# Layer-0 attention: turned keys and P.V sums copied by ScalarE instead of VectorE

## The chip, the core and the metric

One core of a Trainium2 chip runs the whole program. The metric is the device time in microseconds of one execution. Engine names in rows: PE is TensorE (PEld its weight loads), DVE is VectorE, ACT is ScalarE, POOL is GpSimd.

## What is computed

The reference is two transformer-like layers over x of shape (2, 1024, 128). Each layer adds the sum of an attention-like block and a feed-forward block, both fed with the layer-normed x. In layer 0 the two blocks are:

```python
# attention-like block: a small MLP is trained on keys and values, step by step
params, _ = jax.lax.scan(step, (W1, b1, W2, b2), (k, v))   # 1024 gradient steps
q = x @ W_Q
return _mlp(params, q)

# feed-forward block: causal attention with 16 heads of 8, then 4 gated experts
q = _rms(heads(wq), qn_w); k = _rms(heads(wk), kn_w); v = heads(wv)
scores = jnp.einsum('bhqd,bhkd->bhqk', q, k) * HD ** (-0.5)
attn = jax.nn.softmax(jnp.where(causal[None, None], scores, -jnp.inf), axis=-1)
ao = jnp.einsum('bhqk,bhkd->bhqd', attn, v)...
```

Layer 1 has a causal attention with 16 heads of 64 and 8 gated experts. The change concerns the causal attention of layer 0 only, which is the softmax attention over 2 batches, 16 heads, 1024 tokens.

## The kernel before

The program runs in stages: norm and projections (to about 68 us), layer-0 attention together with the training of the small MLP (to about 627 us), the rest of layer 0 (to about 780 us), layer-1 attention and experts (to the end).

The stage of the change works in trips. One trip is one batch and one group of four heads (`HG`), so there are `TRIPS` = 8. A trip has two passes:

- The first pass, `FIRST0`, finds the row maxima. It turns the keys with TensorE transposes (`("tk", half)`, two halves of 512 tokens), turns the queries (`("tq", half)`), multiplies them (`("a", p)`, 48 products), and VectorE takes the maximum of each product (`("mx", p)`, lines 1340 and 1343). The maxima are put beside the queries (`("cb", h)`, line 1346), and the queries are turned again with them (`("tq2", half)`).
- The second pass, `SECOND0`, makes the probabilities: scores again (`("st", n, h)`, 12 blocks of keys by 4 heads, line 1861), an exponential on ScalarE (`("ex", n, h)`, line 964), and the products with the values (`("pv", n)`, line 1878), summed in PSUM bank 6. After blocks 3 and 11 (`LAST`) the sums are complete; they are copied to the tile `ots` (`("oc", half)`, line 1350), turned (`("to", half)`), and VectorE divides them by the sum of the exponentials (`rc` and `zt`, lines 1355 and 1358).

All turns (`tk`, `tq`, `tq2`, `to`, line 1826) write one PSUM bank, `TURN_BANK` = 7, so each waits until the one before has been copied out. The turned keys go to `kta` (`("ka", half)`, line 1327), the turned queries to `qta` and `qtb` by four ScalarE copies of 32 rows each (line 955), each copy from and to the rows 32h to 32h+31 of head h.

In the same queues runs the training of the MLP, one pair of 64-token chunks to a trip: a serial chain of small products (line 1656), a tanh (line 949), and VectorE steps (`sl` line 1242, `grc` line 1251, the differences and their maxima in lines 1295 and 1301 in the first sweep of a chunk, the updates of the state in line 1290).

The order of all this is one written string, `SLOT`, in which every letter takes the next step of the training (`t`), of the first pass of trip s (`f`) or of the second pass of trip s-1 (`s`). Every engine walks the same list and takes what is its own, in that order. Seven full slots run (the first starts near 118 us, the last ends near 587 us); `SLOT_HEAD` before them has no second pass, `SLOT_TAIL` behind them no first pass. The list of one slot begins and ends so:

```python
st.0.0  t.1.base  st.0.1  tk.0  t.1.zc.0  st.0.2  st.0.3  tq.0  copy.tq.0.0  st.1.0  t.1.y.0 ...
... pv.0  tk.1  a.0  a.1  st.2.0  t.1.y.1  a.2  a.3  st.2.1  tq.1 ...
... t.1.zc.4  t.1.kvn  pv.3  a.16  st.5.0  t.1.y.4  st.5.1 ...
... pv.10  tq2.1  copy.tq2.1.0  t.0.dc.4  copy.tq2.1.1  pv.11  copy.tq2.1.2  t.0.up  to.1  copy.tq2.1.3
```

On VectorE a copy stands at `tk` and at `pv.3` and `pv.11`. Who waits for these copies on TensorE (`turn_bank_freed` and `slot`): `tq.0` and `tq.1` wait for `ka` 0 and 1, as the bank has to be free; the products `a` and `st` for the keys; `to.0` and `to.1` for `oc` 0 and 1, and also for the bank; `pv.4` and the next slot's `pv.0` for bank 6.

Of the kernel before, what the change touches and what calls it, by code (L numbers as in the profile page):

```python
# [77 lines left out]
def program(nc, x_in, w0_in, w1_in, out):  # L78
    with ExitStack() as ctx:
# [214 lines left out]
        TURN_BANK = 7  # L294
# [52 lines left out]
        def vector_steps(items):  # L347
            vec = []
            for r in items:
                if r[0] == "tk":  # L350
                    vec.append(("ka", r[1]))
                elif r[0] == "a":
                    vec.append(("mx", r[1]))
                    c, h, i, k = PIECES0[r[1]]
                    if (c, i, k) == (1, TB - 1, 1):
                        vec.append(("cb", h))
                elif r[0] == "pv" and r[1] in LAST:
                    vec.append(("oc", LAST.index(r[1])))
                elif r[0] == "to":
                    vec += [("rc", r[1]), ("zt", r[1])]  # L360
            return vec

        f0_pe = Steps(sem("f0_products"), [r for r in FIRST0 if r[0] != "copy"])
        s0_pe = Steps(sem("s0_products"), SECOND0)
        f0_act = Steps(sem("f0_scalar"), [("qa" if r[1] == "tq" else "qb",) + r[2:] for r in FIRST0 if r[0] == "copy"])
        s0_act = Steps(sem("s0_scalar"), [("ex",) + r[1:] for r in SECOND0 if r[0] == "st"])
        f0_dve = Steps(sem("f0_vector"), vector_steps(FIRST0))
# [521 lines left out]
        def _(act):  # L889
# [47 lines left out]

            def slot(order, s, before):
                for r in order:
# [5 lines left out]
                    elif r[0] == "t" and r[2] == "zc":  # L945
                        _, q, _, k = r
                        src = zh if k else zb
                        wait(act, t_dve, (q, "z", k) if k else (q, "zb"), before if q else s)
                        act.activation(th[:, :, :], src[:, :, :], ACT.Tanh).then_inc(t_act.sem, 1)
                    elif r[0] == "copy":  # L950
                        _, kind, half, h = r
# [14 lines left out]

            slot(SLOT_HEAD, 0, None)
            for i in range(TRIPS // 2 - 1):
                slot(SLOT, i * 2 + 1, i * 2)
                slot(SLOT, i * 2 + 2, i * 2 + 1)  # L970
            slot(SLOT, TRIPS - 1, TRIPS - 2)
            slot(SLOT_TAIL, TRIPS, TRIPS - 1)

# [102 lines left out]
        def _(dve):  # L1076
# [241 lines left out]
            def slot(order, s, before, b, g):  # L1318


                kta_, tmq = kta[:, b, :], tmqs[:, b, :, :]
                for r in order:
                    if r[0] == "t":
                        train_step(before if r[1] else s, *r[1:])
                    elif r[0] == "tk":
                        wait(dve, f0_pe, r, s)
                        dve.tensor_copy(kta_[:, 512 * r[1]:512 * (r[1] + 1)], PS[:, TURN_BANK, :])\
                            .then_inc(f0_dve.sem, 1)
                    elif r[0] == "a":
# [14 lines left out]
                        if (c, i, k) == (1, TB - 1, 1):  # L1344
                            wait(dve, f0_dve, ("mx", r[1]), s)
                            dve.tensor_tensor(tmq[:, 4:8, col], NMH0[:, h, :, 0], NMH0[:, h, :, 1], ALU.min)\
                                .then_inc(f0_dve.sem, 1)
                    elif r[0] == "pv" and r[1] in LAST:
                        wait(dve, s0_pe, r, before)
                        dve.tensor_copy(ots[:, LAST.index(r[1]), :], PS[:, 6, :]).then_inc(s0_dve.sem, 1)  # L1350
                    elif r[0] == "to":
# [278 lines left out]
        def _(pe):  # L1630
# [159 lines left out]
            def turn_bank_freed(order, r, s, before):  # L1790

                turns = [t for t in order if is_turn(t)]
                k = turns.index(r)
                if k == 0:
                    wait(pe, f0_act, ("qb", 1, HG - 1), s, 1)
                    if before is not None:
                        wait(pe, s0_dve, ("zt", 1), before, 1)
                    return
                kind, half = turns[k - 1]
                if kind == "tk":  # L1800
                    wait(pe, f0_dve, ("ka", half), s)
                elif kind == "to":
                    wait(pe, s0_dve, ("zt", half), before)
                else:
                    wait(pe, f0_act, ("qa" if kind == "tq" else "qb", half, HG - 1), s)

            def slot(order, s, before, b):
                for r in order:
                    if r[0] == "t":
                        train_step(before if r[1] else s, *r[1:])  # L1810
                    elif is_turn(r):
# [6 lines left out]
                        elif kind == "tq2":  # L1818

                            wait(pe, f0_dve, ("cb", HG - 1) if half else ("mx", P0_HALF - 1), s)  # L1820
                        elif kind == "to":
                            wait(pe, s0_dve, ("oc", half), before)
                        tm = {"tk": tmk, "to": None}.get(kind, tmqs[:, b, :, :])
# [4 lines left out]
                    elif r[0] == "a":  # L1828
# [5 lines left out]
                        if (i, k) == (4 * c, 0):  # L1834
                            wait(pe, f0_act, ("qa", c, h), s)
                            wait(pe, f0_dve, ("ka", c), s)
                        if p >= 2:
# [6 lines left out]
                    elif r[0] == "st":  # L1844
# [14 lines left out]
                        if n == 0:  # L1859
                            wait(pe, f0_dve, ("ka", 1), before)  # L1860
                        ins = pe.matmul(PS[:, 4 + h % 2, 0:w], kta[:, 1 - b, j * P:(j + 1) * P], qtb[:, h, q0:q0 + w],  # L1861
                                        start=True, stop=True)
                        ins.then_inc(s0_pe.sem, 1)
                    elif r[0] == "pv":
# [4 lines left out]
                        if n == 0:  # L1869
                            pe.wait_ge(s0_values, before + 1)  # L1870
                            wait(pe, s0_dve, ("oc", 1), before, 1)
                        elif j == 0:
                            wait(pe, s0_dve, ("oc", 0), before)
                        if n in DIAG0:
# [284 lines left out]
```

## Time and profile before

| what | us |
|---|---|
| runs | 1507.38, 1503.93, 1507.27; median 1507.27 |
| the profiled execution | 1505.46 |
| its span, first to last instruction | 1503.7 |
| PE busy | 1383.7 (92%) |
| DVE busy | 1103.2 (73%) |
| ACT busy | 784.8 (52%) |

The page gives the busy time of each engine over the span. The views named below read the trace of the same execution: stretches of time with the busy time of each engine, waits by pair of lines, groups of instructions by line and form, and the timeline of one engine, in which a row has its start, its duration, and in brackets the idle time before it with what ended it. A row with "x4" merges four instructions in a row; its duration is that of all four.

### The profile page before, as it was taken

What the parts mean: (1) busy time and instruction counts of PE and PEld (TensorE: products, weight loads), DVE (VectorE), ACT (ScalarE), POOL (GpSimd) and SP (SyncE); (2) the same over time, 40 slices, a digit from 0 to 9 for tenths busy, and PEclk for the clock granted to TensorE, in tenths of its full rate; (3) what the DMA queues carried; (4) which work ended last, traced back from release to release, by engine and by line L of the source; (5) the groups of instructions that cost most, each with busy time, mean ns of one, the idle gap of its engine ahead of it and who ended that gap; (6) DMA issues with size and microseconds to landing.
All of it is one profiled execution on the core that took longest, in us unless ns stands there. A gap on an engine that the chain in (4) does not pass through costs nothing.

```text
span 1503.7 us, 27515 instructions
## 1 busy us (share of the span) xinstructions
PE 1383.7 (92%) x9204; PEld 1055.9 (70%) x9204; DVE 1103.2 (73%) x3389; ACT 784.8 (52%) x1701; POOL 280.3 (19%) x413
## 2 busy tenths in 40 slices
PE   4189999999999999889949999999999999989998
PEld 2167677777767776656627777788787777768887
DVE  3788888989888887452247778887878877855555
ACT  3315464555546555443327666666667666633322
POOL 4001011111101101000043323322222333400000
PEclk9589999999999999989979999999999999989999
DMA  2000000000000000300000000000000000000000
GB/s 96 0 2 1 1 1 1 2 1 1 1 1 2 1 2 1 137 5 0 0 14 1 1 2 1 1 2 1 1 1 2 1 2 1 1 1 1 0 0 28
DMA packets 5612, 12.02 MB, mean 8 GB/s; under 512 B 112, under 2 KB 5232, under 8 KB 5232
## 3 DMA queue, kind: packets, MB, share of 16 engines
q1 hardware_dynamic: 5488, 10.44, 1.9%
q8 instruction: 69, 1.13, 0.3%
q14 instruction: 55, 0.45, 0.1%
HBM read 9.39 MB, written 1.05 MB: 7 GB/s over the span
## 4 chain that ended last, share of the span: by engine, by line
PE 56%; DVE 4%; POOL 1%; ACT 1%; issue 1%; DVEq 0%; ACTq 0%; POOLq 0%
PE PS L2019 9%; PE PS L2033 8%; PE PS L2087 6%; PE PS L2012 5%; PE PS L2011 5%; PE PS L1960 5%; PE PS L2100 4%; PE PS L2046 4%; PE PS L2053 4%; PE PS L1980 2%; PE PS L2061 2%; PE PS L1656 2%; PE PS L1861 1%; PE PS L1878 1%; PE PS L1935 1%
## 5 line engine op out<-in xcount | busy, mean ns | idle before, releaser
L964 ACT ACTIVATE pe_<-PS 128x512 f32<-128x512 f32 (+3 forms) x384 | 176.0, 488 | 152.7 <-PE PS L1861 151.3
L1031 ACT ACTIVATE PN<-PS,NM 128x128 f32<-128x128 f32 (+7 forms) x256 | 189.7, 742 | 106.5 <-DVE NM L1529 52.3
L1529 DVE CUSTOM_DVE_ANT_0 PS<-PS,mask_row 128x128 f32<-128x128 f32 (+7 forms) x256 | 192.6, 773 | 41.9 <-PE PS L2012 38.2
L2011 PE MATMUL PS<-KA,QA 128*128 128x512 f32 (+3 forms) x384 | 161.5, 420 | 15.2 <-DVE KA L1568 14.4
L2019 PE MATMUL PS<-ident,PN 128*128 128x128 f32 x1152 | 170.8, 276 | 1.6 <-ACT PN L1031 1.5
L1841 PE MATMUL PS<-kta,qta 128*128 128x512 f32 (+3 forms) x384 | 146.0, 411 | 7.3 <-DVE tmqs L1340 2.4
L2019 PEld LDWEIGHTS PS<-ident,PN 128*128 128x128 f32 x1152 | 131.8, 141 | 27.7 <-issue 17.4
L1861 PE MATMUL PS<-qtb,kta 128*128 128x512 f32 (+3 forms) x384 | 136.3, 385 | 1.0 <-ACT pe_ L964 0.9
L2012 PE MATMUL PS<-KB,QA 128*128 128x512 f32 (+3 forms) x384 | 129.1, 348 | 0.0
L1340 DVE CUSTOM_DVE_ANT_0 PS<-PS,W 128x128 f32<-128x128 f32 (+3 forms) x256 | 124.7, 496 | 3.6 <-PE PS L1841 2.3
L786 POOL TENSOR_SCALAR_AFFINE_SELECT pe_<-pe_ 128x512 f32<-128x512 f32 x64 | 40.8, 637 | 407.2 <-ACT pe_ L964 407.2
L2011 PEld LDWEIGHTS PS<-KA,QA 128*128 128x128 f32 x384 | 73.6, 192 | 33.4 <-DVE QA L1565 14.5
L1841 PEld LDWEIGHTS PS<-kta,qta 128*128 128x128 f32 x384 | 70.8, 193 | 33.3 <-issue 9.9
L1861 PEld LDWEIGHTS PS<-qtb,kta 128*128 128x128 f32 x384 | 68.6, 190 | 34.3 <-ACT pe_ L964 24.8
L850 POOL CAST KA<-RAW 64x512 fp32r<-64x512 f32 x64 | 46.3, 723 | 243.9 <-ACT RAW L1053 241.5
L1343 DVE TENSOR_REDUCE NMH<-PS 128x1 f32<-128x512 f32 x128 | 87.9, 687 | 4.1 <-PE PS L1841 4.1
L2087 PE MATMUL PS<-QA,w_s 128*128 128x512 f32 x256 | 83.6, 408 | 5.4 <-DVE w_s L1594 5.2
L856 POOL TENSOR_TENSOR KB<-RAW,KA 64x512 fp32r<-64x512 f32 x64 | 87.2, 1363 | 4.4
L1070 ACT ACTIVATE pe_<-PS 128x512 f32<-128x512 f32 x64 | 38.0, 598 | 86.3 <-PE PS L2087 45.7
L2012 PEld LDWEIGHTS PS<-KB,QA 128*128 128x128 f32 x384 | 74.1, 193 | 12.6 <-issue 7.1
L1878 PE MATMUL PS<-pe_,arena 128*32 128x512 f32 (+3 forms) x768 | 81.8, 498 | 0.0
L1039 ACT ACTIVATE PTB<-PS 128x512 f32<-128x512 f32 (+2 forms) x144 | 64.7, 483 | 30.2 <-PE PS L2019 29.2
(253 smaller groups left out, 3103.7 us busy)
## 6 DMA issues: line engine op xcount, KB each, us to landing
W<-w SPq DMA_DIRECT2D x1, 5124.0 KB, 15.8
W<-w SPq DMA_DIRECT2D x1, 2508.0 KB, 10.8
X<-x SPq DMA_DIRECT2D x2, 512.0 KB, 4.8
out<-X SPq DMA_DIRECT2D x1, 1024.0 KB, 5.1
WOZ<-w SPq DMA_DIRECT2D x2, 256.0 KB, 4.2
```

Source lines behind the costliest of these rows:

```text
L964: act.activation(pe_[:, h, n % 2, 0:w], PS[:, 4 + h % 2, 0:w], ACT.Exp, scale=HD0 ** -0.5)\
L1031: act.activation(prob_rows(u, r), scores_of(u), ACT.Exp, bias=NM[:, u:u + 1], scale=-1.0, accum_out=SM[:, r % 2, u:u + 1]).then_inc(score_ ...
L1340: dve.tensor_tensor_reduce(piece, piece, mask_row0[:, 512 - w:512], -1.0, -MASKED, ALU.add, ALU.min, dst).then_inc(f0_dve.sem, 1)
L1529: dve.tensor_tensor_reduce(scores_of(u), scores_of(u), mask_row[:, S - w:S], -HD1 ** -0.5, -MASKED, ALU.add, ALU.min, NM[:, u:u + 1]).then ...
L1841: ins = pe.matmul(PS[:, bank, 0:w], qta[:, h, i * P:(i + 1) * P], kta[:, b, 512 * k:512 * k + w], start=True, stop=True)
L1861: ins = pe.matmul(PS[:, 4 + h % 2, 0:w], kta[:, 1 - b, j * P:(j + 1) * P], qtb[:, h, q0:q0 + w], start=True, stop=True)
L1878: ins = pe.matmul(PS[32 * h:32 * h + 32, 6, q0 - 512 * c:512], tmv[:, j, 32 * h:32 * h + 32], pe_[:, h, n % 2, 0:512 * (c + 1) - q0], star ...
L2011: pe.matmul(piece, query, KA[:, b, h, lo:lo + n], start=True, stop=False)
L2012: ins = pe.matmul(piece, query, KB[:, b, h, lo:lo + n], start=False, stop=True)
L2019: ins = pe.transpose(PS[:, ring_bank[item, r], (j - 4 * k) * P:(j - 4 * k + 1) * P], prob_rows(u, r)[:, j * P:(j + 1) * P], ident[:, :])
L2033: ins = pe.matmul(PS[head_rows(h), Z_BANK, lo:n], VS[:, b, j, head_rows(h)], probs(g, r)[:, h, j, lo:n], start=(j == 0), stop=(j == hi_til ...
L2087: ins = pe.matmul(PS[:, 2 * (u % 3) + a, :], w[:, k, part, half * P:(half + 1) * P], xs[:, cols], start=(i == 0), stop=(i == 2))
```

## The change

Four copies of each trip change engine. `ka` 0 and 1 (two copies of 128 x 512 from PSUM to `kta`) and `oc` 0 and 1 (two of 128 x 512 from PSUM to `ots`) leave VectorE's queue and join ScalarE's, at the same places of the written order. TensorE waits on ScalarE's counters for them. Nothing else moves: TensorE's and GpSimd's instructions and their order stay the same. Over the program 32 copies move, four in each of 8 trips.

```diff
--- before.py
+++ after.py
@@ -347,23 +347,21 @@
         def vector_steps(items):
             vec = []
             for r in items:
-                if r[0] == "tk":
-                    vec.append(("ka", r[1]))
-                elif r[0] == "a":
+                if r[0] == "a":
                     vec.append(("mx", r[1]))
                     c, h, i, k = PIECES0[r[1]]
                     if (c, i, k) == (1, TB - 1, 1):
                         vec.append(("cb", h))
-                elif r[0] == "pv" and r[1] in LAST:
-                    vec.append(("oc", LAST.index(r[1])))
                 elif r[0] == "to":
                     vec += [("rc", r[1]), ("zt", r[1])]
             return vec
 
         f0_pe = Steps(sem("f0_products"), [r for r in FIRST0 if r[0] != "copy"])
         s0_pe = Steps(sem("s0_products"), SECOND0)
-        f0_act = Steps(sem("f0_scalar"), [("qa" if r[1] == "tq" else "qb",) + r[2:] for r in FIRST0 if r[0] == "copy"])
-        s0_act = Steps(sem("s0_scalar"), [("ex",) + r[1:] for r in SECOND0 if r[0] == "st"])
+        f0_act = Steps(sem("f0_scalar"), [("ka", r[1]) if r[0] == "tk" else ("qa" if r[1] == "tq" else "qb",) + r[2:]
+                                          for r in FIRST0 if r[0] in ("copy", "tk")])
+        s0_act = Steps(sem("s0_scalar"), [("oc", LAST.index(r[1])) if r[0] == "pv" else ("ex",) + r[1:]
+                                          for r in SECOND0 if r[0] == "st" or r[0] == "pv" and r[1] in LAST])
         f0_dve = Steps(sem("f0_vector"), vector_steps(FIRST0))
         s0_dve = Steps(sem("s0_vector"), vector_steps(SECOND0))
         s0_keys, s0_queries, s0_values = sem("a0_keys_staged"), sem("a0_queries_staged"), sem("a0_values_staged")
@@ -935,7 +933,7 @@
             act.wait_ge(first_kv, 1)
             act.copy(kvs[:, 0, :, :], PS[:, 1, :].rearrange("p (a n) -> p a n", a=4)).then_inc(first_copy, 1)
 
-            def slot(order, s, before):
+            def slot(order, s, before, b):
                 for r in order:
                     if r[0] == "t" and r[2] == "kvn":
                         q = r[1]
@@ -947,6 +945,12 @@
                         src = zh if k else zb
                         wait(act, t_dve, (q, "z", k) if k else (q, "zb"), before if q else s)
                         act.activation(th[:, :, :], src[:, :, :], ACT.Tanh).then_inc(t_act.sem, 1)
+                    elif r[0] == "tk":
+                        wait(act, f0_pe, r, s)
+                        act.copy(kta[:, b, 512 * r[1]:512 * (r[1] + 1)], PS[:, TURN_BANK, :]).then_inc(f0_act.sem, 1)
+                    elif r[0] == "pv" and r[1] in LAST:
+                        wait(act, s0_pe, r, before)
+                        act.copy(ots[:, LAST.index(r[1]), :], PS[:, 6, :]).then_inc(s0_act.sem, 1)
                     elif r[0] == "copy":
                         _, kind, half, h = r
                         dst = qta if kind == "tq" else qtb
@@ -964,12 +968,12 @@
                         act.activation(pe_[:, h, n % 2, 0:w], PS[:, 4 + h % 2, 0:w], ACT.Exp, scale=HD0 ** -0.5)\
                             .then_inc(s0_act.sem, 1)
 
-            slot(SLOT_HEAD, 0, None)
+            slot(SLOT_HEAD, 0, None, 0)
             for i in range(TRIPS // 2 - 1):
-                slot(SLOT, i * 2 + 1, i * 2)
-                slot(SLOT, i * 2 + 2, i * 2 + 1)
-            slot(SLOT, TRIPS - 1, TRIPS - 2)
-            slot(SLOT_TAIL, TRIPS, TRIPS - 1)
+                slot(SLOT, i * 2 + 1, i * 2, 1)
+                slot(SLOT, i * 2 + 2, i * 2 + 1, 0)
+            slot(SLOT, TRIPS - 1, TRIPS - 2, 1)
+            slot(SLOT_TAIL, TRIPS, TRIPS - 1, 0)
 
 
             for c in range(NC):
@@ -1318,14 +1322,10 @@
             def slot(order, s, before, b, g):
 
 
-                kta_, tmq = kta[:, b, :], tmqs[:, b, :, :]
+                tmq = tmqs[:, b, :, :]
                 for r in order:
                     if r[0] == "t":
                         train_step(before if r[1] else s, *r[1:])
-                    elif r[0] == "tk":
-                        wait(dve, f0_pe, r, s)
-                        dve.tensor_copy(kta_[:, 512 * r[1]:512 * (r[1] + 1)], PS[:, TURN_BANK, :])\
-                            .then_inc(f0_dve.sem, 1)
                     elif r[0] == "a":
                         c, h, i, k = PIECES0[r[1]]
                         wait(dve, f0_pe, r, s)
@@ -1345,9 +1345,6 @@
                             wait(dve, f0_dve, ("mx", r[1]), s)
                             dve.tensor_tensor(tmq[:, 4:8, col], NMH0[:, h, :, 0], NMH0[:, h, :, 1], ALU.min)\
                                 .then_inc(f0_dve.sem, 1)
-                    elif r[0] == "pv" and r[1] in LAST:
-                        wait(dve, s0_pe, r, before)
-                        dve.tensor_copy(ots[:, LAST.index(r[1]), :], PS[:, 6, :]).then_inc(s0_dve.sem, 1)
                     elif r[0] == "to":
                         c = r[1]
                         wait(dve, s0_pe, r, before)
@@ -1798,7 +1795,7 @@
                     return
                 kind, half = turns[k - 1]
                 if kind == "tk":
-                    wait(pe, f0_dve, ("ka", half), s)
+                    wait(pe, f0_act, ("ka", half), s)
                 elif kind == "to":
                     wait(pe, s0_dve, ("zt", half), before)
                 else:
@@ -1819,7 +1816,7 @@
 
                             wait(pe, f0_dve, ("cb", HG - 1) if half else ("mx", P0_HALF - 1), s)
                         elif kind == "to":
-                            wait(pe, s0_dve, ("oc", half), before)
+                            wait(pe, s0_act, ("oc", half), before)
                         tm = {"tk": tmk, "to": None}.get(kind, tmqs[:, b, :, :])
                         for i in range(4):
                             src = tm[:, 4 * half + i, :] if tm is not None else ots[:, half, i * P:(i + 1) * P]
@@ -1833,7 +1830,7 @@
                         bank = 2 + p % 2
                         if (i, k) == (4 * c, 0):
                             wait(pe, f0_act, ("qa", c, h), s)
-                            wait(pe, f0_dve, ("ka", c), s)
+                            wait(pe, f0_act, ("ka", c), s)
                         if p >= 2:
                             wait(pe, f0_dve, ("mx", p - 2), s)
                         else:
@@ -1857,7 +1854,7 @@
                         if j == 0:
                             wait(pe, f0_act, ("qb", c, h), before)
                         if n == 0:
-                            wait(pe, f0_dve, ("ka", 1), before)
+                            wait(pe, f0_act, ("ka", 1), before)
                         ins = pe.matmul(PS[:, 4 + h % 2, 0:w], kta[:, 1 - b, j * P:(j + 1) * P], qtb[:, h, q0:q0 + w],
                                         start=True, stop=True)
                         ins.then_inc(s0_pe.sem, 1)
@@ -1868,9 +1865,9 @@
                         q0 = max(512 * c, P * j)
                         if n == 0:
                             pe.wait_ge(s0_values, before + 1)
-                            wait(pe, s0_dve, ("oc", 1), before, 1)
+                            wait(pe, s0_act, ("oc", 1), before, 1)
                         elif j == 0:
-                            wait(pe, s0_dve, ("oc", 0), before)
+                            wait(pe, s0_act, ("oc", 0), before)
                         if n in DIAG0:
                             pe.wait_ge(s0_masked, len(DIAG0) * before + DIAG0.index(n) + 1)
                         for h in range(HG):
```

The moved copies stand in the queues as follows. In these rows `th` is the tanh, `qta` and `qtb` are turned queries, `pe_` the exponentials, `sl`, `grc` and `cmax` tiles of the training. First ScalarE's queue from the end of one full slot to the start of the next, before:

```order
L964 ACTIVATE pe_<-PS 128x128 x4
L955 CAST qtb<-PS 32x512 x4
L964 ACTIVATE pe_<-PS 128x512 x2
L949 ACTIVATE th<-zb 128x256
L964 ACTIVATE pe_<-PS 128x512 x2
L955 CAST qta<-PS 32x512
L964 ACTIVATE pe_<-PS 128x384 x2
L955 CAST qta<-PS 32x512 x3
```

and now:

```order
L968 ACTIVATE pe_<-PS 128x128 x4
L959 CAST qtb<-PS 32x512 x2
L953 COPY ots<-PS 128x512
L959 CAST qtb<-PS 32x512 x2
L968 ACTIVATE pe_<-PS 128x512 x2
L950 CAST kta<-PS 128x512
L947 ACTIVATE th<-zb 128x256
L968 ACTIVATE pe_<-PS 128x512 x2
L959 CAST qta<-PS 32x512
L968 ACTIVATE pe_<-PS 128x384 x2
L959 CAST qta<-PS 32x512 x3
```

`oc` 1 stands between the second and the third copy of the last turned queries, and `ka` 0 between the exponentials and the tanh that begins a chunk.

VectorE's queue at the start of a full slot, before:

```order
L1230 SCALAR_TENSOR_TENSOR vb<-kvs,st 128x128
L1327 CAST kta<-PS 128x512
L1242 SCALAR_TENSOR_TENSOR sl<-th,zb 128x128 x2
L1295 TENSOR_TENSOR grc<-grc 128x256
L1301 TENSOR_REDUCE cmax<-grc 128x4
L1251 SCALAR_TENSOR_TENSOR grc<-PS,vb 128x128
```

and now:

```order
L1234 SCALAR_TENSOR_TENSOR vb<-kvs,st 128x128
L1246 SCALAR_TENSOR_TENSOR sl<-th,zb 128x128 x2
L1299 TENSOR_TENSOR grc<-grc 128x256
L1305 TENSOR_REDUCE cmax<-grc 128x4
L1255 SCALAR_TENSOR_TENSOR grc<-PS,vb 128x128
```

The copy of the keys stood ahead of the two products that use the tanh; they now follow the set-up of the chunk directly.

VectorE's queue behind the second turn of the keys, before:

```order
L1242 SCALAR_TENSOR_TENSOR sl<-th,zh 128x128 x2
L1327 CAST kta<-PS 128x512
L1340 ISA PS,tmqs<-PS,W 128x128
L1340 ISA tmqs 128x1
L1340 ISA PS,tmqs<-PS,W 128x256
```

and now:

```order
L1246 SCALAR_TENSOR_TENSOR sl<-th,zh 128x128 x2
L1340 ISA PS,tmqs<-PS,W 128x128
L1340 ISA tmqs 128x1
L1340 ISA PS,tmqs<-PS,W 128x256
L1340 ISA tmqs 128x1
```

The maxima (`ISA PS,tmqs`) now follow the training step without the copy between.

## Rows read from the trace of the kernel before

**Rows 1.** The page, busy time, share of the span and count by engine.

```profile
PE 1383.7 (92%) x9204; PEld 1055.9 (70%) x9204; DVE 1103.2 (73%) x3389; ACT 784.8 (52%) x1701; POOL 280.3 (19%) x413
```

**Rows 2.** Stretches: the third full slot. Length, then busy (count) of PE, PEld, DVE, ACT, POOL, granted clock.

```profile
252.10:319.10 67.00, 65.30 (x464) 48.29 (x462) 58.97 (x220) 36.00 (x76) 8.77 (x20) 1.00 0.01 1
```

**Rows 3.** Waits, 119 to 586 us: who waited for whom, us in total, times, longest.

```profile
PE PS L1826 <- DVE tmqs L1346: 4.7, 7, 0.7
...
PE PS L1656 <- DVE grc L1251: 2.8, 7, 0.4
```

**Rows 4.** Groups by line and form, 110 to 600 us: busy us, mean ns | idle before.

```profile
L955 ACT CAST qtb<-PS 32x512 fp32r<-32x512 f32 x60 | 34.6, 577 | 19.8 <-PE PS L1826 18.7
...
L1327 DVE CAST kta<-PS 128x512 fp32r<-128x512 f32 x14 | 9.6, 688 | 1.1 <-PE PS L1826 0.3
...
L943 ACT COPY kvs<-PS 128x512 f32<-128x512 f32 x15 | 8.7, 578 | 0.1
```

**Rows 5.** Timeline, PE, end of the third slot and start of the fourth: start us, duration us.

```profile
315.54 0.63 PE L1826 MATMUL PS<-ident,tmqs 128*128 128x128 f32 x4 [0.67 <-DVE tmqs L1346]
...
318.34 0.28 PE L1656 MATMUL PS<-ones,grc 128*128 128x1 f32 x2
318.63 0.66 PE L1826 MATMUL PS<-ident,ots 128*128 128x128 f32 x4
...
321.61 0.66 PE L1826 MATMUL PS<-ident,tmqs 128*128 128x128 f32 x4 [0.22 <-DVE kta L1327]
...
323.46 0.49 PE L1656 MATMUL PS<-grc 128*128 128x128 f32 x2 [0.40 <-DVE grc L1251]
```

**Rows 6.** Timeline, ACT, the same stretch.

```profile
316.20 2.38 ACT L955 CAST qtb<-PS 32x512 fp32r<-32x512 f32 x4 [1.53 <-PE PS L1826]
...
320.73 0.41 ACT L949 ACTIVATE th<-zb 128x256 f32<-128x256 f32 x1
321.04 1.08 ACT L964 ACTIVATE pe_<-PS 128x512 f32<-128x512 f32 x2
```

**Rows 7.** Timeline, DVE, the same stretch.

```profile
317.03 0.69 DVE L1350 COPY ots<-PS 128x512 f32<-128x512 f32 x1
...
320.87 0.68 DVE L1327 CAST kta<-PS 128x512 fp32r<-128x512 f32 x1
321.47 0.48 DVE L1242 SCALAR_TENSOR_TENSOR sl<-th,zb 128x128 f32<-128x128 f32 x2
...
322.33 0.69 DVE L1301 TENSOR_REDUCE cmax<-grc 128x4 f32<-128x512 f32 x1
323.12 0.29 DVE L1251 SCALAR_TENSOR_TENSOR grc<-PS,vb 128x128 f32<-128x128 f32 x1
```

**Rows 8.** Timeline, PE's weight loads after the second key turn of the third slot.

```profile
261.99 0.19 PEld L1841 LDWEIGHTS PS<-kta,qta 128*128 128x128 f32 x1 [0.20 <-DVE tmqs L1340]
262.10 0.19 PEld L1861 LDWEIGHTS PS<-qtb,kta 128*128 128x128 f32 x1
262.33 0.48 PEld L1826 LDWEIGHTS PS<-ident,tmqs 128*128 128x128 f32 x4
...
263.44 0.19 PEld L1861 LDWEIGHTS PS<-qtb,kta 128*128 128x128 f32 x1
263.92 0.19 PEld L1841 LDWEIGHTS PS<-kta,qta 128*128 128x128 f32 x1 [0.29 <-DVE tmqs L1340]
```

**Rows 9.** Timeline, all engines, the same place, its two rows on DVE.

```profile
260.60 0.69 DVE L1327 CAST kta<-PS 128x512 fp32r<-128x512 f32 x1
...
261.21 0.29 DVE L1340 CUSTOM_DVE_ANT_0 PS<-PS,W 128x128 f32<-128x128 f32 x1
```

**Rows 10.** Timeline, ACT, around the first copy of the P.V sums, third slot.

```profile
277.20 0.59 ACT L943 COPY kvs<-PS 128x512 f32<-128x512 f32 x1
278.22 0.60 ACT L964 ACTIVATE pe_<-PS 128x512 f32<-128x512 f32 x1 [0.44 <-PE PS L1861]
```

**Rows 11.** Timeline, PE, end of the last, partial slot.

```profile
624.99 0.63 PE L1826 MATMUL PS<-ident,ots 128*128 128x128 f32 x4
```

## The prediction, made before the changed kernel ran

> **What bounds the kernel now.** I read the page first: TensorE is busy for 92% of the span, VectorE for 73%, ScalarE for 52% [rows 1]. A share of the span says little here, since the change touches one stage. So I took the stretches next, one for each of the seven full slots of layer-0 attention. They are alike; one stands in [rows 2]. In 67.0 us TensorE's products are busy for 65.3 us, VectorE for 59.0 us (88%), ScalarE for 36.0 us (54%), at the full granted clock. TensorE has 1.7 us without a product in a slot, so whatever the copies did, a slot cannot lose much more than that. The slots make up 7 x 67 = 469 us of the program.
>
> The waits say who holds TensorE up. Two pairs come back once in each slot: 0.67 us for the last row maxima and 0.40 us for a training step [rows 3]. The timeline puts them at their places [rows 5]: 0.67 us at 315.54, ahead of the last turn of the queries (`tq2.1`); 0.40 us at 323.46 (the training step `ds.0`); and 0.22 us at 321.61, where `tq.0` waits for the first key copy. Only this last one is a wait for a moved copy itself. The other gaps are shorter, mostly late weight loads.
>
> TensorE is therefore the bound, with a few fixed places in each slot at which another engine is last. A moved copy is worth what it does at the next such place. I go through the four copies.
>
> **What moves.** A copy took 0.69 us on VectorE; the one ScalarE copy of this shape in the stage, 128 x 512 out of PSUM, takes 0.58 us [rows 4]. Four copies a slot are 2.8 us off VectorE and 2.3 us onto ScalarE, which has 31 us idle. Busy time is not the question, the place in the queue is.
>
> **The second copy of the sums (`oc` 1), at the slot's end.** Before, VectorE did it at 317.03 [rows 7], beside ScalarE's four copies of turned queries. Those run from 316.20 to 318.58 [rows 6], 0.60 us from start to start, though one lasts 0.577 us [rows 4]: they do not overlap at all. The turn `to.1` needs the bank that the last of them empties, and starts at 318.63; TensorE's own work ahead of it ends at 318.34 + 0.28 = 318.62 [rows 5]. ScalarE and TensorE reach this point together, so anything put into ScalarE's row of four shows in full. The change puts `oc` 1 between the second and the third. Its neighbours change rows of partitions as they do among themselves, so I give it their 0.60 us: `to.1` starts at 319.23, and all behind it follows. VectorE's state updates come earlier, but the next chunk's first products stand behind `to.1` in TensorE's queue, so nothing wins this back. **+0.60 us a slot**; bounds 0.48 us (the spacing of two full-height exponentials, 1.08 - 0.60 [rows 6]) and 0.69 us (what it took on VectorE).
>
> The Trainium skill (ScalarE: Activation LUTs, What ACT_TABLE_LOAD costs) says that back-to-back ACTIVATEs overlap by about 93 ns. The full-height exponentials of [rows 6] agree, the 32-row copies do not. By the rule this term would be about 0.49 us, and the whole sum 0.8 us less.
>
> **The first key copy (`ka` 0), at the slot's start.** Before: VectorE from 320.87, then the two `sl` products from 321.47 [rows 7], after the tanh of 320.73, which ends at 321.14 [rows 6]. So `sl` waited for the copy, not for the tanh. Now the copy stands ahead of the tanh on ScalarE, where the exponentials follow each other without a gap. The tanh moves by 0.48 us, to 321.21, and ends at 321.62; `sl` starts near 321.67 instead of 321.47. From there a chain on VectorE, with the maximum of differences (0.69 us, 322.33), leads to `grc` at 323.12 [rows 7], for which TensorE already waits 0.40 us. It is 0.20 us later. The 0.22 us that `tq.0` waited for the copy go, but TensorE only reaches the longer wait sooner. **+0.20 us**; bounds -0.22 us (that wait goes and nothing takes its place) and +0.48 us (the tanh's delay in full). Behind the tanh the exponentials and query copies move by 0.2 us as well, with TensorE.
>
> **The second key copy (`ka` 1).** VectorE did it at 260.60 and the first maximum behind it came at 261.21 [rows 9]. TensorE had two late weight loads for that: 0.20 us at 261.99 and 0.29 us at 263.92 [rows 8]. The load behind a product of the same kind comes after 0.23 us where nothing is late (262.10 to 262.33), after 0.48 us at 263.44 to 263.92: 0.25 us lost there, and about half of 0.20 us at the other, since that load hides in part behind a product. With the copy gone VectorE is up to 0.61 us (261.21 - 260.60) ahead of TensorE, and both waits fall away. ScalarE, idle for 31 us of the slot, has room for the copy between exponentials. **-0.35 us**; bounds 0 (the loads hidden anyway) and -0.61 us (VectorE's lead in full).
>
> **The first copy of the sums (`oc` 0).** On ScalarE it follows the copy of 277.20 at about 277.7 and is nearly over when the next exponential's input is ready; ScalarE was idle for 0.44 us there [rows 10]. TensorE has no wait for VectorE of note near it. **0**; bounds -0.10 and +0.10 us (a quarter of that idle time, either way).
>
> **Sum.** 0.60 + 0.20 - 0.35 + 0 = +0.45 us a slot, times 7 = +3.1 us. In the head slot only the key copies exist and ScalarE is nearly idle: -0.3 us, as for `ka` 1. In the tail no query copies stand in ScalarE's row and `to.1` at 624.99 [rows 11] follows TensorE's own work: 0. Together **+2.8 us, 0.19%**. Against the profiled execution, 1505.46 us, that gives 1508.3 us; against the median of the runs, 1507.27 us, 1510.1 us. The profiled run lies 1.8 us under the median, and I take the middle, **1509 us**. Some 0.3% (4.5 us) is what a measurement of this kernel can tell from no change.
>
> Range: all lower ends, 0.48 - 0.22 - 0.61 - 0.10 = -0.45 us a slot, give -3.2 us, 1502.3 us on the profiled run; all upper ends, 0.69 + 0.48 + 0 + 0.10 = 1.27 us, give +8.9 us, 1516.2 us on the median.
>
> **Rivals.**
>
> *ScalarE's queue holds the training chain up (slower).* The place is the tanh behind `ka` 0. If its whole delay of 0.48 us reaches TensorE, because the exponentials and query copies behind it form one row without a gap and feed later steps late, and if VectorE's lead after `ka` 1 wins nothing, a slot costs 0.60 + 0.48 = 1.08 us: +7.6 us, about 1514 us (between 1513 and 1515). From 0.64 us a slot on it passes 4.5 us. For it: that row runs from the slot's start to the copies of `tq.0`. Against it: `sl` had 0.33 us of slack behind the tanh (321.47 - 321.14).
>
> *VectorE is the bound, and its relief is the gain (faster).* At 88% it is the busiest engine of the slot but for TensorE's products. If its 2.8 us carried over to every place at which TensorE waits for it, 0.67 + 0.40 + 0.22 = 1.29 us would go, -9.0 us; with `oc` 1 at +0.60 us, -4.8 us, about 1501 us. Against it: VectorE falls idle for the tanh and for products between the copies and the 0.67 us wait, so a lead won at 277 us is gone long before 315 us. The Trainium skill (Perfetto Trace Analysis, Identifying the Most-Contended Engine) wants occupancy for VectorE and the share of weight loads for TensorE, and the most contended engine optimized first. By [rows 2] that compares 59.0 us of VectorE with 48.3 us of PEld, so by that rule VectorE is the engine to relieve, which is this rival. The order of the waits speaks against it.
>
> **How the numbers follow.** Forecast (a small loss, under 4.5 us) 0.63; the slower rival 0.28; the faster rival 0.09. Faster by over 0.3%: 0.09; within 0.3%: 0.63; slower by over 0.3%: 0.28. The range is 1502.5 to 1516.
>
> **What would show it.** In the new profile the slots should be 67.4 to 67.5 us long. At the slot's end ScalarE should show two query copies, the copy of the sums, two query copies, some 3.0 us in all, and `to.1` right behind them. At the start the tanh should come 0.5 us after the key copy and the wait for `grc` be 0.6 us or more, with none at `tq.0`. The loads of [rows 8] should come without a wait. The 0.67 us ahead of `tq2.1` should still be there. If it is gone, or the slots are shorter than 67.0 us, I am wrong about which engine binds; over 67.65 us, about the tanh.

## The result, and the profile after

The changed kernel takes 1509.3 us (median; 1507.4 to 1514.2), the kernel before 1506.6 us on the same chips. The ratio is 1.0021, with a 95% interval from 1.0013 to 1.0029: slower by 0.2%, below the 0.3% taken as the bound. The profiled execution took 1507.93 us, with a span of 1506.2 us.

The stretches of the changed kernel, third full slot, answer to [rows 2]; the columns are the same.

```profile
253.50:321.00 67.50, 65.19 (x464) 48.19 (x462) 57.03 (x214) 37.83 (x80) 8.74 (x20) 1.00 0.01 1
```

VectorE is busy for 1.9 us less in a slot, ScalarE for 1.8 us more. Both are less than the 2.8 us and 2.3 us of the copies' durations, since a row starts before the one ahead of it has ended. TensorE's products need the same 65 us; the slot is longer. Its length to a hundredth comes from TensorE's timeline, from one first score product (`st.0.0`) to the next. Before:

```profile
252.11 0.48 PE L1861 MATMUL PS<-qtb,kta 128*128 128x512 f32 x1
...
319.05 0.48 PE L1861 MATMUL PS<-qtb,kta 128*128 128x512 f32 x1
```

That is 66.94 us. The changed kernel's timeline of TensorE has these rows; `L1858` is the old `L1861`, `L1823` the old `L1826`, `L1653` the old `L1656`:

```profile
253.55 0.48 PE L1858 MATMUL PS<-qtb,kta 128*128 128x512 f32 x1
...
316.86 0.63 PE L1823 MATMUL PS<-ident,tmqs 128*128 128x128 f32 x4 [0.67 <-DVE tmqs L1346]
...
319.66 0.28 PE L1653 MATMUL PS<-ones,grc 128*128 128x1 f32 x2
320.56 0.66 PE L1823 MATMUL PS<-ident,ots 128*128 128x128 f32 x4 [0.62 <-ACT qtb L959]
320.97 0.48 PE L1858 MATMUL PS<-qtb,kta 128*128 128x512 f32 x1
...
323.29 0.66 PE L1823 MATMUL PS<-ident,tmqs 128*128 128x128 f32 x4
324.09 0.44 PE L1858 MATMUL PS<-qtb,kta 128*128 128x384 f32 x1
...
325.59 0.49 PE L1653 MATMUL PS<-grc 128*128 128x128 f32 x2 [0.43 <-DVE grc L1255]
```

The slot takes 67.42 us, 0.48 us more. The others agree: from `to.1` to `to.1` the second to sixth slots take 66.92 to 66.94 us before and 67.42 to 67.46 us now, the seventh 66.74 and 67.24 us. Only the first grew by more, from 67.06 to 67.84 us. Against [rows 5] three things are to be seen. The 0.67 us for the last maxima, at 316.86, is untouched. The turn `to.1` at 320.56 now stands 0.62 us idle for a ScalarE query copy, where before there was no gap. And `tq.0` at 323.29 no longer waits for the key copy. ScalarE's timeline of the same stretch shows why `to.1` waits, and answers to [rows 6]:

```profile
317.52 1.18 ACT L959 CAST qtb<-PS 32x512 fp32r<-32x512 f32 x2 [1.53 <-PE PS L1823]
318.72 0.58 ACT L953 COPY ots<-PS 128x512 f32<-128x512 f32 x1
319.33 1.18 ACT L959 CAST qtb<-PS 32x512 fp32r<-32x512 f32 x2
...
322.66 0.58 ACT L950 CAST kta<-PS 128x512 fp32r<-128x512 f32 x1
323.12 0.43 ACT L947 ACTIVATE th<-zb 128x256 f32<-128x256 f32 x1
```

The row from 317.52 to 319.33 + 1.18 = 320.51 takes 2.99 us where it took 2.38 us, and `to.1` starts 0.05 us behind it. The tanh starts 0.46 us after the key copy. VectorE's timeline, against [rows 7]:

```profile
323.58 0.49 DVE L1246 SCALAR_TENSOR_TENSOR sl<-th,zb 128x128 f32<-128x128 f32 x2 [0.71 <-ACT th L947]
...
325.24 0.29 DVE L1255 SCALAR_TENSOR_TENSOR grc<-PS,vb 128x128 f32<-128x128 f32 x1
```

From the slot's start to `sl` it is now 323.58 - 320.97 = 2.61 us, before 321.47 - 319.05 = 2.42 us: 0.19 us more, with VectorE idle for the tanh. Behind the second key turn the weight loads of TensorE, against [rows 8], read:

```profile
263.17 0.30 PEld L1838 LDWEIGHTS PS<-kta,qta 128*128 128x128 f32 x2
263.46 0.19 PEld L1858 LDWEIGHTS PS<-qtb,kta 128*128 128x128 f32 x1
263.69 0.47 PEld L1823 LDWEIGHTS PS<-ident,tmqs 128*128 128x128 f32 x4
...
265.20 0.19 PEld L1838 LDWEIGHTS PS<-kta,qta 128*128 128x128 f32 x1 [0.29 <-DVE tmqs L1340]
```

The first late load is gone (two loads in a row at 263.17), the second stays.

### The profile page after: what moved, and what is told of

Same layout as the page of the kernel before. It is cut to its first block, busy times and chain, and to the rows that moved or that the text cites. A ratio compares the mean times of both kernels' runs of the same rounds, so it can differ in the third digit from the quotient of the medians.

```text
span 1506.2 us, 27515 instructions
## 1 busy us (share of the span) xinstructions
PE 1381.0 (92%) x9204; PEld 1052.5 (70%) x9204; DVE 1086.6 (72%) x3357; ACT 799.2 (53%) x1733; POOL 279.6 (19%) x413
## 4 chain that ended last, share of the span: by engine, by line
PE 56%; DVE 4%; ACT 1%; POOL 1%; issue 1%; DVEq 0%; ACTq 0%; POOLq 0%
PE PS L2016 9%; PE PS L2030 8%; PE PS L2084 6%; PE PS L2009 5%; PE PS L1957 5%; PE PS L2008 4%; PE PS L2097 4%; PE PS L2043 4%; PE PS L2050 4%; PE PS L1977 2%; PE PS L2058 2%; PE PS L1653 2%; PE PS L1858 1%; PE PS L1875 1%; PE PS L1932 1%
## 5 line engine op out<-in xcount | busy, mean ns | idle before, releaser
L1858 PE MATMUL PS<-qtb,kta 128*128 128x512 f32 (+3 forms) x384 | 136.5, 386 | 2.0 <-ACT pe_ L968 0.9
L1858 PEld LDWEIGHTS PS<-qtb,kta 128*128 128x128 f32 x384 | 68.5, 190 | 37.0 <-ACT pe_ L968 27.4
```

## The experiments

Two theories stood against each other. By the theory of places a moved copy costs or saves only what it does at its own place in the two queues. By the theory of load it is the sum of work on ScalarE and VectorE that counts, so each copy has a like share of the result. Five kernels, one of them measured twice, decide between them by choosing, copy by copy, the engine. They differ from the changed kernel by this helper and by one list; each engine's walk and TensorE's waits ask it:

```diff
+        ON_ACT = [("pv", LAST[1])]
+
+        def copied(r, by_act):
+            return (r[0] == "tk" or r[0] == "pv" and r[1] in LAST) and (r in ON_ACT) == by_act
...
-                    elif r[0] == "tk":
+                    elif r[0] == "tk" and copied(r, True):
                         wait(act, f0_pe, r, s)
...
+                    elif r[0] == "tk" and copied(r, False):
+                        wait(dve, f0_pe, r, s)
+                        dve.tensor_copy(kta[:, b, 512 * r[1]:512 * (r[1] + 1)], PS[:, TURN_BANK, :])\
+                            .then_inc(f0_dve.sem, 1)
...
-                            wait(pe, s0_act, ("oc", half), before)
+                            wait(pe, s_oc[half], ("oc", half), before)
```

The kernel's whole time scatters by a few microseconds from the stages outside the full slots: the first full slot starts anywhere from 118.1 to 121.1 us in these traces. In the head slot the granted clock differs from trace to trace; from 86 to 90 us it was 0.51 before and 1.00 in the changed kernel. Of all this the edits touch only the key copies of the head slot and the copies of the sums in the last, partial slot. The third slot's length, read from `st.0.0` to `st.0.0`, repeats within 0.03 us in the kernels that ran twice. So the slots carry the argument, and the ratios say what is left of it in the whole. In the rows below, `...` stands for rows left out.

**Only `oc` 1 on ScalarE.** `ON_ACT = [("pv", LAST[1])]`, as above.

> Only the second copy of the P.V sums (oc 1) is on ScalarE, the other three copies stay on VectorE. Theory of places (each copy acts only at its own place in the queue): all of the loss is here, a slot takes 66.93 + 0.61 = 67.54 us, the kernel is 4.3 us slower than before (ratio 1.0028). Theory of load (each copy on ScalarE costs about the same, 0.50 / 4 = 0.12 us): a slot takes 67.05 us, 0.9 us slower, no difference to be measured.

The ratio is 1.0032 (1.0023 to 1.0041), the slot 67.52 us. TensorE's timeline:

```profile
255.13 0.48 PE L1877 MATMUL PS<-qtb,kta 128*128 128x512 f32 x1
...
322.24 0.66 PE L1842 MATMUL PS<-ident,ots 128*128 128x128 f32 x4 [0.63 <-ACT qtb L971]
322.65 0.48 PE L1877 MATMUL PS<-qtb,kta 128*128 128x512 f32 x1
```

One copy alone makes +0.58 us a slot, and more than the whole loss in time. The theory of load, with a quarter of 0.50 us, falls.

**All but `oc` 1 on ScalarE.**

```diff
-        ON_ACT = [("pv", LAST[1])]
+        ON_ACT = [("tk", 0), ("tk", 1), ("pv", LAST[0])]
```

> Three copies on ScalarE, only oc 1 back on VectorE. Theory of places: +0.19 (ka 0) - 0.35 (ka 1) + 0.04 (oc 0) = -0.12 us a slot, 66.8 us, the kernel 0.8 us faster than before, within what can be told from no change. Theory of load: three quarters of the loss stay, 67.3 us a slot, 2.6 us slower than before.

The ratio is 1.0001 (0.9992 to 1.0010), the slot 66.84 us (253.94 to 320.78): 0.10 us less than before. Putting one copy back on VectorE takes 0.58 us off the changed kernel's slot, and with it all of the loss.

```profile
253.94 0.48 PE L1877 MATMUL PS<-qtb,kta 128*128 128x512 f32 x1
...
320.37 0.66 PE L1842 MATMUL PS<-ident,ots 128*128 128x128 f32 x4
320.78 0.48 PE L1877 MATMUL PS<-qtb,kta 128*128 128x512 f32 x1
```

In TensorE's timeline `to.1` at 320.37 has no wait any more.

**Only `ka` 1 on ScalarE, twice.** `ON_ACT = [("tk", 1)]`.

> Only the second key copy (ka 1) is on ScalarE. Theory of places: VectorE is free 0.6 us earlier behind the second turn of the keys, a slot takes 66.93 - 0.35 = 66.58 us, the kernel is 2.4 us faster than before (ratio 0.9984). Theory of load: 67.05 us a slot. If the gain of ka 1 depends on ka 0 having gone too, it lies between.

The slot is 66.64 us (253.06 to 319.70), 0.30 us less than before, as the theory of places has it within 0.06 us. The ratio did not follow: 0.9999 (0.9990 to 1.0008), where seven such slots make 0.9986. So it ran again.

> The kernel with only ka 1 on ScalarE once more, since its slots were 0.30 us shorter than before (2.1 us in seven) and its time was not (ratio 0.9999, interval 0.9990 to 1.0008). If that was scatter of the stages outside the slots, the slots are 66.63 us again and the ratio comes nearer to 0.9986. If the gain in the slots is given back behind them, the ratio is 1.000 again, and the stretch from the last full slot's end to the end of the program is about 2 us longer than before.

Now the ratio is 0.9987 (0.9978 to 0.9996), with a slot of 66.61 us (252.77 to 319.38). The two profiled executions have the same span to 0.1 us (1501.8 and 1501.7 us, before 1503.7 us). Nothing is given back behind the slots: from the end of the seventh to the end of the program the two take 915.8 and 916.0 us, before 917.1 us. So the first measurement's ratio is put down to scatter; its typical execution was slower than the profiled one (1505.9 against 1503.9 us), and no trace of such an execution was kept. TensorE's timeline of the first of the two:

```profile
253.06 0.48 PE L1877 MATMUL PS<-qtb,kta 128*128 128x512 f32 x1
...
319.70 0.48 PE L1877 MATMUL PS<-qtb,kta 128*128 128x512 f32 x1
```

Its weight loads show the same pattern as the changed kernel's: the first late load gone, the second still there.

```profile
262.48 0.30 PEld L1857 LDWEIGHTS PS<-kta,qta 128*128 128x128 f32 x2
...
264.52 0.19 PEld L1857 LDWEIGHTS PS<-kta,qta 128*128 128x128 f32 x1 [0.29 <-DVE tmqs L1359]
```

**Only `ka` 0 on ScalarE.** `ON_ACT = [("tk", 0)]`.

> Only the first key copy (ka 0) is on ScalarE, ahead of the tanh. Theory of places: the tanh comes 0.47 us later, the products behind it 0.2 us later, a slot takes 67.12 us, the kernel 1.3 us slower than before. Rival: what counts is the wait of 0.22 us of the query turn for this copy, which goes; then a slot takes 66.71 us, 1.5 us faster.

The slot is 67.13 us (255.05 to 322.18), 0.19 us more than before. The ratio is 1.0021 (1.0011 to 1.0030); seven slots account for 1.0009, and the rest lies outside them. TensorE's timeline:

```profile
255.05 0.48 PE L1877 MATMUL PS<-qtb,kta 128*128 128x512 f32 x1
...
257.38 0.66 PE L1842 MATMUL PS<-ident,tmqs 128*128 128x128 f32 x4
258.18 0.44 PE L1877 MATMUL PS<-qtb,kta 128*128 128x384 f32 x1
...
259.68 0.49 PE L1672 MATMUL PS<-grc 128*128 128x128 f32 x2 [0.43 <-DVE grc L1267]
```

`tq.0` comes sooner, without its wait, but the training step comes 259.68 - 255.05 = 4.63 us after the slot's start instead of 323.46 - 319.05 = 4.41 us. The exact size differs by 0.02 us with the slot taken. The rival, by which the removed wait is what counts, falls.

**Only `oc` 0 on ScalarE.** `ON_ACT = [("pv", LAST[0])]`.

> Only the first copy of the P.V sums (oc 0) is on ScalarE. Theory of places: nothing waits near it, a slot takes 66.93 us within 0.05 us, the time is that of before. Theory of load: 67.05 us a slot.

The slot is 66.90 us (253.46 to 320.36), the ratio 1.0005 (0.9997 to 1.0014): nothing, as expected. ScalarE's timeline shows the copy between the copy of the next keys and the next exponential, each starting half a microsecond after the one before:

```profile
278.55 0.58 ACT L953 COPY kvs<-PS 128x512 f32<-128x512 f32 x1
279.03 0.59 ACT L965 COPY ots<-PS 128x512 f32<-128x512 f32 x1
279.56 0.60 ACT L980 ACTIVATE pe_<-PS 128x512 f32<-128x512 f32 x1
```

**The key copy behind the tanh, twice.** As all but `oc` 1, and ScalarE alone walks the order with `("tk", 0)` moved behind the tanh:

```diff
+            def key_copy_behind_tanh(order):
+                items, i = list(order), order.index(("tk", 0))
+                tanh = next(j for j in range(i, len(items)) if items[j][0] == "t" and items[j][2] == "zc")
+                items.insert(tanh, items.pop(i))
+                return items
...
-                for r in order:
+                for r in key_copy_behind_tanh(order) if ("tk", 0) in order else order:
```

> As with three copies on ScalarE (oc 1 on VectorE), and in ScalarE's queue the first key copy stands behind the tanh instead of ahead of it. Theory of places: the tanh is at its old time, and as VectorE has no key copy either, the products behind it start 0.3 us earlier than in the kernel before; the query turn waits some 0.3 us for the copy instead of 0.22 us. A slot takes 66.93 - 0.3 - 0.35 = 66.3 us, the kernel is 4.5 us faster than before (ratio 0.997). Rival (the tanh was not what held the chain up): as three copies on ScalarE, 66.8 us a slot, 0.8 us faster.

The ratio is 0.9987 (0.9975 to 0.9998), the slot 66.43 us (254.37 to 320.80), 0.51 us less than before and 0.41 us less than with the copy ahead of the tanh. The expected 66.3 us is missed by 0.13 us. TensorE's timeline says where:

```profile
254.37 0.48 PE L1883 MATMUL PS<-qtb,kta 128*128 128x512 f32 x1
...
257.00 0.66 PE L1848 MATMUL PS<-ident,tmqs 128*128 128x128 f32 x4 [0.28 <-ACT kta L968]
...
258.55 0.49 PE L1678 MATMUL PS<-grc 128*128 128x128 f32 x2
```

The training step starts 4.18 us after the slot's start and no longer waits: of the 0.40 us that this step waited before, 0.23 us are gained; the rest is TensorE's own work and the wait of 0.28 us at 257.00 for the key copy. VectorE's `sl` starts right behind the tanh:

```profile
256.50 0.49 DVE L1264 SCALAR_TENSOR_TENSOR sl<-th,zb 128x128 f32<-128x128 f32 x2 [0.23 <-ACT th L965]
```

It ran once more.

> The fastest version so far (three copies on ScalarE, the first key copy behind the tanh) once more: slots of 66.43 us, 3.5 us less than before over the seven, ratio 0.9977. If slots that are shorter are paid for behind them, as the ratio of 0.9987 in the first measurement may hint, it is 0.999 again.

The slot is 66.44 us again (252.01 to 318.45); the ratio is 0.9991 (0.9979 to 1.0003), where seven slots make 0.9977. The first interval reaches 0.9977, the second begins at 0.9979, so the gain in the slots is not fully found in the time. The head slot shows where much of the rest goes. Its first key turn (`tk.0`), the query turn behind it and the first product `a` stand so in TensorE's timeline, with the tanh from ScalarE's:

```profile
69.50 1.09 PE L1848 MATMUL PS<-ident,arena 128*128 128x128 f32 x4 [4.48 <-POOL arena L778]
...
72.22 0.42 ACT L965 ACTIVATE th<-zb 128x256 f32<-128x256 f32 x1 [6.75 <-DVE zb L1250]
...
73.16 1.12 PE L1848 MATMUL PS<-ident,tmqs 128*128 128x128 f32 x4 [1.72 <-ACT kta L968]
...
77.51 0.77 PE L1863 MATMUL PS<-kta,qta 128*128 128x128 f32 x2
```

Before, in TensorE's timeline:

```profile
69.02 1.09 PE L1826 MATMUL PS<-ident,arena 128*128 128x128 f32 x4 [4.48 <-POOL arena L768]
...
75.34 0.78 PE L1841 MATMUL PS<-kta,qta 128*128 128x128 f32 x2
```

There the tanh comes late, the key copy now waits for it, and `tq.0` waits 1.72 us for the copy. From `tk.0` to the first `a` it takes 77.51 - 69.50 = 8.01 us, before 75.34 - 69.02 = 6.32 us: 1.7 us lost once. The seven slots together are 3.2 us shorter in both traces, since the first gains less than the others. That leaves 1.5 us, a ratio of 0.9990 by estimate, inside both intervals. How much of the 1.7 us is still there at the end of the head slot can't be read, because the granted clock changes in between. The two profiled executions have spans of 1506.9 and 1501.7 us, with equal slots; what sets them apart lies outside the slots. It is the version with the shortest slots, and in time level with the one that moves `ka` 1 alone (1503.4 us both in the last comparison, before 1505.6 us).

**The last query copies all from row 0.** The changed kernel, with one edit. It alters part of the computation: the probabilities of heads 1 to 3 for the queries 512 to 1023 come from head 0's queries.

```diff
-                        rows = slice(32 * h, 32 * h + 32)
+                        rows = slice(32 * h, 32 * h + 32) if (kind, half) != ("tq2", 1) else slice(0, 32)
```

> The changed kernel, all four copies on ScalarE, but the four copies of the last turned queries (tq2, second half) all go from and to rows 0 to 31, so the probabilities of the heads 1 to 3 for the queries 512 to 1023 are computed from head 0's queries: that part of the computation is changed. Theory (copies do not overlap because the start row changes): the five copies of the row start 0.48 us apart instead of 0.60 us, the row takes 2.5 us instead of 3.0 us, the turn behind it comes 0.5 us earlier, a slot takes 66.93 us, the kernel is 3.5 us faster than the changed one. Rival (32-row copies never overlap, or copies to fp32r do not): the row takes 3.0 us, a slot 67.43 us, as the changed kernel.

The ratio to before is 0.9996 (0.9988 to 1.0005), 1505.6 us against 1509.3 us for the changed kernel, and the slot is 66.94 us (253.06 to 320.00). ScalarE's timeline:

```profile
317.03 1.05 ACT L971 CAST qtb<-PS 32x512 fp32r<-32x512 f32 x2 [1.53 <-PE PS L1842]
317.99 0.57 ACT L965 COPY ots<-PS 128x512 f32<-128x512 f32 x1
318.47 1.06 ACT L971 CAST qtb<-PS 32x512 fp32r<-32x512 f32 x2
```

and TensorE's:

```profile
319.17 0.28 PE L1672 MATMUL PS<-ones,grc 128*128 128x1 f32 x2
319.58 0.66 PE L1842 MATMUL PS<-ident,ots 128*128 128x128 f32 x4
```

Same number of copies, same sizes, same types: with one start row the whole row takes 319.53 - 317.03 = 2.50 us instead of 2.99 us, and `to.1` starts 0.13 us behind TensorE's own work, which ends at 319.45. The 0.49 us is as much as the whole loss of the change in a slot, but it is not the price of `oc` 1 alone: the four query copies, too, stand closer than before. At the closer spacing the fifth copy still adds 0.48 us to the row; the change of start row makes it 0.60 us. The edit changes the start row on the PSUM side and on the SBUF side together, so which of the two counts is open.

## Why the prediction was right

The time forecast was 1509 us, 1509.3 us was measured; the forecast +2.8 us (0.19%) stands beside 0.21% in the ratio. The case was the forecast one, a small loss. That the totals agree so closely is in part luck: in the traces the seven slots grew by 3.8 us (468.5 to 472.2 us), not 3.1 us, and the spans differ by only 2.5 us, because the stages behind the slots took 1.5 us less (917.1 and 915.7 us; in all traces they take 915.5 to 920.6 us). By its steps, each as the difference between the two traces from one product of TensorE to another in a slot: `oc` 1 from `tq2.1` to `to.1` (318.63 - 315.54 = 3.09 us before, 320.56 - 316.86 = 3.70 us now), `ka` 0 from the slot's start to the training step (256.53 - 252.11 = 4.42 us before, 258.16 - 253.55 = 4.61 us now), `ka` 1 from that step to the first product of the fourth key block (`st.3.0`; 266.69 - 256.53 = 10.16 us before, 267.97 - 258.16 = 9.81 us now), `oc` 0 what is left between there and `tq2.1`. "Alone" is the slot's length in the kernel with that copy alone on ScalarE, against 66.94 us:

| step | predicted | in the change | alone |
|---|---|---|---|
| `oc` 1 | +0.60 us | +0.61 us | +0.58 us |
| `ka` 0 | +0.20 us | +0.19 us | +0.19 us |
| `ka` 1 | -0.35 us | -0.35 us | -0.30 us |
| `oc` 0 | 0 | +0.04 us | -0.04 us |
| a slot | +0.45 us | +0.48 us | +0.43 us (sum) |

The four steps of the change add up to 0.49 us; the last 0.01 us, from `to.1` to the slot's end, is rounding.

**`oc` 1.** Mechanism and size held. That ScalarE and TensorE reach `to.1` together was read from two ends 0.04 us apart, and the price followed from the spacing of the neighbours. The rule of the Trainium skill (ScalarE: Activation LUTs, What ACT_TABLE_LOAD costs), an overlap of about 93 ns between ACTIVATEs, would have given 0.49 us, an estimate. It holds for copies that start at the same row, as the last experiment shows (0.48 us from start to start for 0.57 us of duration), and not where the start row changes, as here. What the experiment adds is that the change of start row is what keeps the copies from overlapping, which the prediction had assumed without a test.

**`ka` 0.** The size held, but one sentence did not: with its wait gone, `tq.0` was to reach the longer wait sooner, so that this wait would be 0.6 us or more. It is 0.43 us. TensorE is held in between as well: the product behind `tq.0` starts at 324.09, 0.80 us after it, where before it came 0.41 us after it (322.02 behind 321.61), since its PSUM bank waits for an exponential that stands behind the tanh. The tanh's delay reaches TensorE on two paths, and both come out near 0.2 us, so the sum was not hurt. That the tanh was the cause is shown by the version that moves the copy behind it. In the first full slot the size failed: `ka` 0 alone makes it 67.53 us instead of 67.06 us, 0.47 us, near the upper bound. There the tanh had no slack to begin with: it ended at 120.22 + 0.42 = 120.64 us before, and `sl` started at 120.67. In the change the step comes 0.48 us later there (122.67 - 118.12 = 4.55 us, now 123.32 - 118.29 = 5.03 us), which is why the first slot grew by more than the others.

**`ka` 1.** The size held and its parts did not. I had both late loads fall away, the first for about 0.10 us and the second for 0.25 us. The first one fell away, for 0.22 us. In TensorE's timeline, before and now:

```profile
261.61 0.88 PE L1841 MATMUL PS<-kta,qta 128*128 128x384 f32 x2
262.33 0.28 PE L1861 MATMUL PS<-qtb,kta 128*128 128x256 f32 x1
```

```profile
263.19 0.66 PE L1838 MATMUL PS<-kta,qta 128*128 128x384 f32 x2
263.69 0.28 PE L1858 MATMUL PS<-qtb,kta 128*128 128x256 f32 x1
```

The two products take 262.33 - 261.61 = 0.72 us before, 263.69 - 263.19 = 0.50 us now. The second one stayed at 0.29 us, with 0.08 us gained on the way there (263.92 - 262.33 = 1.59 us, now 265.20 - 263.69 = 1.51 us); the remaining 0.05 us lie ahead of the pair. VectorE did not keep its lead. Counted from the slot's start, its first maximum came 0.35 us earlier than before (262.30 - 253.55 against 261.21 - 252.11), the one behind the four operations of the training step only 0.16 us earlier (263.88 - 253.55 against 262.60 - 252.11). Those operations stand between the maxima in its own queue and are the likely brake; no kernel moved them. That two wrong parts made the right sum is luck.

**`oc` 0, head and tail.** Nothing near `oc` 0, as said. The -0.3 us for the head slot is not borne out. From `tk.0` to the first `a` the head slot takes 77.10 - 70.58 = 6.52 us instead of 6.32 us, so `ka` 0 costs 0.2 us there too, a part that this term left out. What `ka` 1 gave there cannot be seen: the first full slot starts at 118.29 us instead of 118.12 us, within a scatter of 3 us from trace to trace. The tail did not change.

**The rivals.** The slower rival wanted 1.08 us a slot; the tanh's slack of 0.33 us on VectorE was real and `ka` 1 gave its 0.35 us. The faster rival wanted the 0.67 us ahead of `tq2.1` to shrink; it reads 0.67 us in both traces. VectorE lost 1.9 us of work a slot, and its most expensive wait did not move, as the prediction argued from VectorE's idle times in between. The prediction's opening holds TensorE's 1.7 us without a product for the most that a slot can lose; they limit only how much shorter a slot can get, not how much longer. No term of the sum uses that sentence. The rule to relieve the most contended engine first (the Trainium skill, Perfetto Trace Analysis, Identifying the Most-Contended Engine) would have named VectorE. Here occupancy did not tell what a copy is worth, its place did.

## What to carry to other kernels

When work is moved to an idle engine, look up the place it lands in, not the idle share: here an engine idle for 31 us of a 67 us slot had one row of copies that ended just when TensorE needed it, and a copy put into that row cost all of its time. Move one piece at a time where pieces are independent: `ka` 1 gained 0.30 us a slot, `oc` 0 did nothing, `ka` 0 cost 0.19 us, and `oc` 1, at 0.58 us, cost more than the whole change. Where the step that starts a serial chain is ready, a short copy belongs behind it: that gave 0.41 us a slot here. Where that step comes late, as in the head slot, the copy waits with it, 1.7 us here.

## What was not expected of the hardware

ScalarE's copies of 32 rows overlap by about 0.1 us when they start at the same row (0.48 us from start to start), and not at all when the start row changes from one instruction to the next (0.60 us from start to start, 0.577 us each). A full-height copy between two of them behaves in the same way: it starts at row 0, and it overlapped when its neighbours did too (317.99 to 318.47, 0.48 us) and not when they started elsewhere (318.72 to 319.33, 0.61 us).
